# First keys in one VectorE instruction, two groups' keys spread from ScalarE's queue, the last down product in halves, and a new order of all pieces

## The reference

```python
x = x + attn_a(ln(x))   # W: 16 query heads, 2 key/value heads, window: query t sees keys t-16..t+15
x = x + ffn(ln(x))      # F: expand to 512, 9 butterfly stages, gelu, 9 butterfly stages, contract to 128
x = x + attn_b(ln(x))   # L: linear attention, phi = elu + 1
x = x + ffn(ln(x))      # G: the same weights as F
```

## Time and profile before

| | |
|---|---|
| runs of the kernel before | 549.33 us median of 3 (547.2, 549.33, 549.78) |
| profiled execution, its own time | 548.77 us |
| its span, first to last instruction | 547.0 us |
| TensorE busy | 514.8 us, 94% |
| GpSimd busy | 449.6 us, 82% |
| VectorE busy | 424.4 us, 78% |
| ScalarE busy | 356.5 us, 65% |
| granted TensorE clock | 0.999 |

### The profile page before, as it was taken

One profiled execution on the slowest core, in us unless ns is written; L12 is line 12 of the kernel. 1 busy time (PEld: TensorE's weight loads), 2 busy tenths in 40 slices (PEclk: granted clock), 3 DMA queues, 4 the chain that ended last, 5 costly groups with the idle time before them and its releaser, 6 DMA issues.

```text
span 547.0 us, 14353 instructions
## 1 busy us (share of the span) xinstructions
PE 514.8 (94%) x5060; PEld 337.4 (62%) x5060; DVE 424.4 (78%) x1272; ACT 356.5 (65%) x578; POOL 449.6 (82%) x640
## 2 busy tenths in 40 slices
PE   4788989999999999999999999999999999999996
PEld 2454344756667676666676676766576676767764
DVE  4978888997978888887888888888878687745451
ACT  2654457576768777776767686776777777747542
POOL 6548789999989999898998989999979796797240
PEclk9999999999999999999999999999999999999999
DMA  8433323231322212131423222231422312110001
GB/s 305 153 100 85 101 63 84 59 79 46 103 50 79 60 46 76 43 102 38 103 50 105 49 59 74 61 85 40 118 64 63 72 27 59 31 29 20 1 20 40
DMA packets 49543, 38.87 MB, mean 71 GB/s; under 512 B 12352, under 2 KB 38976, under 8 KB 49472
## 3 DMA queue, kind: packets, MB, share of 16 engines
q1 hardware_dynamic: 47024, 33.73, 24.4%
q10 hardware_dynamic: 2448, 4.22, 2.2%
HBM read 15.64 MB, written 5.51 MB: 39 GB/s over the span
## 4 chain that ended last, share of the span: by engine, by line
PE 61%; POOL 19%; DVE 5%; issue 5%; DMA 5%; SPq 3%; ACT 2%; POOLq 0%; DVEq 0%; ACTq 0%
PE ring L785 15%; PE ring L773 14%; POOL probs_t L602 7%; PE ring L715 6%; PE ps_s L741 6%; PE ring L796 4%; PE ps_o L758 4%; PE ring L816 3%; PE ring L866 2%; DMA probs_t<-probs_t 2%; SPq L446 2%; PE ring L843 2%; PE ring L805 1%; DMA x_P<-in_x 1%; POOL xb_W L572 1%
## 5 line engine op out<-in xcount | busy, mean ns | idle before, releaser
L602 POOL TENSOR_TENSOR probs_t<-probs_t,first 128x1024 f32<-128x1024 f32 x64 | 151.4, 2376 | 19.3 <-DMA probs_t<-probs_t 19.1
L785 PEld LDWEIGHTS ring<-w,early 128*128 128x128 f32 x1024 | 118.9, 192 | 10.8 <-issue 8.5
L1189 ACT ACTIVATE early<-ring,b 128x512 f32<-128x512 f32 x128 | 84.3, 685 | 62.2 <-PE ring L773 61.8
L785 PE MATMUL ring<-w,early 128*128 128x128 f32 x1024 | 119.8, 275 | 1.8 <-ACT early L1189 1.6
L1180 ACT ACT_TABLE_LOAD x58 | 74.4, 1283 | 10.1 <-issue 9.1
L1198 ACT ACTIVATE probs_t<-merged_t 128x1024 f32<-128x1024 f32 x64 | 65.8, 1044 | 11.4 <-DVE merged_t L1547 9.3
L741 PE MATMUL ps_s<-kx,q_t 64*32 64x512 f32 x960 | 64.7, 596 | 2.9 <-DVE merged L1540 1.6
L1555 DVE STREAM_TRANSPOSE ps_o<-ps_o 128x512 f32<-128x512 f32 x64 | 46.1, 721 | 21.3 <-PE ps_o L758 21.3
L773 PE MATMUL ring<-xT_G,w1b 128*128 128x512 f32 x128 | 60.8, 595 | 0.7 <-ACT xT_G L1170 0.7
L773 PE MATMUL ring<-xT_F,w1b 128*128 128x512 f32 x128 | 60.1, 608 | 0.4 <-ACT xT_F L1170 0.3
L1528 DVE COPY_PREDICATED ps_s<-first,ps_s 128x512 f32<-128x512 uint32 x64 | 43.9, 687 | 15.9 <-PE ps_s L741 14.7
(11 more groups left out here) (124 smaller groups left out, 985.7 us busy)
## 6 DMA issues: line engine op xcount, KB each, us to landing
probs_t<-probs_t SPq DMA_DIRECT2D x256, 64.0 KB, 2.0
kx<-kv_rows SPq DMA_DIRECT2D x120, 40.0 KB, 2.1
x_P<-in_x SPq DMA_DIRECT2D x16, 256.0 KB, 3.3
out_x<-x_G SPq DMA_DIRECT2D x16, 256.0 KB, 2.5
vx_t<-kv_rows SPq DMA_DIRECT2D x128, 8.0 KB
up_s<-in_up_m ACTq DMA_DIRECT2D x7, 256.0 KB, 7.9
down_s<-in_down_m ACTq DMA_DIRECT2D x7, 256.0 KB, 8.1
kv_rows<-kv_t SPq DMA_DIRECT2D x16, 80.0 KB, 2.8
```

The source lines that it names most:

```text
L602: nc.gpsimd.tensor_tensor(parts, parts, keep.rearrange("p (a t) -> p a t", a=1).to_broadcast([P, PAIR * HEADS, WIN]), ALU.mult).then_inc(p ...
L785: last = nc.tensor.matmul(bank(name)[:, P * j:P * (j + 1)], hid[s][:, c, P * j:P * (j + 1)], w2[:, c], start=(c == 0), stop=(c == CH - 1))
L1189: nc.scalar.activation(hid[s][:, c], bank(name)[:], ACT.Gelu, bias=b1[:, c:c + 1]).then_inc(drained[BANK[name]].sem, 1)
```

## The change

- **First keys.** The first half of group 0's keys (`X.ka`) is written by one VectorE instruction over 8 x 288 elements, with the head mask as a broadcast second operand; the second half (`X.kb`) by 8 ScalarE instructions. A new column `bk_row` holds the bias.
- **Clearing.** GpSimd clears half of `kx` (128x2560 instead of 128x5120), ScalarE the other half by one instruction (`clear_keys`). The ones of `v_ext` are set later.
- **Loads.** The 7 loads of `down_s` go out on SyncE's queue, behind `vx_t`, instead of between those of `up_s` on ScalarE's queue.
- **Keys of groups 1 and 2** (the second and third group) are spread by 8 DMAs each from ScalarE's queue; those of the other groups stay on SyncE's.
- **Last down product.** `G.down` of group 15 puts tiles 0 and 1 into the bank of its first hidden chunk, waits for each hidden chunk just ahead of its first use, and is followed by two residuals and two stores of 128 KB.
- **Order.** Every table and every `turn` is rewritten; the repeated stretch is now that of groups 4 to 12. Some results go to another bank: `W.proj` to `ring2` (was `ring1`), `L.xT` to `ring1` (was `ring0`).

```diff
-            nc.gpsimd.memset(kx[:], 0.0).then_inc(kx_cleared, 1)
-            nc.gpsimd.memset(v_ext[:], 1.0).then_inc(ones_set, 1)
+            nc.gpsimd.memset(kx[:, 0:HPK // 2], 0.0).then_inc(kx_cleared, 1)
+            def set_ones():
+                nc.gpsimd.memset(v_ext[:], 1.0).then_inc(ones_set, 1)
...
+            def spread_keys(g):
+                act.wait_ge(kv_out.sem, kv_out.after(g, "P.ko"))
+                if g == 1:
+                    act.wait_ge(kx_cleared, 2)
+                else:
+                    act.wait_ge(product.sem, product.after(g - 1, *SCORES))
+                for h in range(HPK):
+                    act.dma_start(kx[h:P:HPK, h].rearrange("d (j n) -> d j n", j=TILES), keys_of(g)
+                                 ).then_inc(kx_in.sem, 16)
...
+            def clear_keys():
+                act.wait_ge(kv_cleared, 1)
+                later_keys = kx[:, HPK // 2:HPK].rearrange("p h n -> p (h n)")
+                zeros = x_tp[:, 0:1, 0:PAD]
+                nc.scalar.activation(later_keys.rearrange("p (a n) -> p a n", n=PAD),
+                                     zeros.to_broadcast([P, HPK * TILES * TSPAN // (2 * PAD), PAD]), ACT.Copy).then_inc(kx_cleared, 1)
...
-                for h in range(HPK):
-                    last = nc.vector.tensor_scalar(kx_0[:, h, TPB * TSPAN + PAD:TILES * TSPAN - PAD],
-                                                   bank("X.kb")[:, PAD:TPB * TSPAN - PAD], head_s[:, h:h + 1],
-                                                   bk_head[:, h:h + 1], ALU.mult, ALU.add)
-                last.then_inc(drained[BANK["X.kb"]].sem, 1)
+                width = TPB * TSPAN - 2 * PAD
+                nc.vector.scalar_tensor_tensor(
+                    kx_0[:, :, PAD:TPB * TSPAN - PAD],
+                    bank("X.ka")[:, PAD:TPB * TSPAN - PAD].rearrange("p (a n) -> p a n", a=1).to_broadcast([P, HPK, width]), bk_row,
+                    head_s.rearrange("p (h a) -> p h a", a=1).to_broadcast([P, HPK, width]), ALU.add, ALU.mult
+                ).then_inc(drained[BANK["X.ka"]].sem, 1)
...
+                ends = ends_apart(g, s)
...
                 for j in range(TILES):
+                    if ends and j == TILES // 2:
+                        last.then_inc(first_tiles, 1)
+                        free(g, name)
+                    sums = bank(f"{s}.up{chunks[0]}" if ends and j < TILES // 2 else name)
+                    for c in chunks:
+                        if j == 0 and ends:
+                            ready = drained[BANK[f"{s}.up{c}"]]
+                            pe.wait_ge(ready.sem, ready.after(g, f"{s}.up{c}"))
...
-    ("P.xT", 0, "0", 0, 0), ("X.u0a", 0, "2", 0, 0), ("X.u0b", 0, "3", 0, 0), ("X.ka", 0, "0", 0, 0),
+    ("P.xT", 0, "0", 0, 0), ("X.u0a", 0, "1", 0, 0), ("X.u0b", 0, "2", 0, 0), ("X.ka", 0, "0", 0, 0),
```

More of the change, by code:

```diff
@@ L186 @@
+    ("P.kv", "bank"), ("P.q", "P.xT"), ("W.PV1", "values"), ("W.PV2", "values"), ("W.PV3", "values"), ("W.S1", "P.q"),
[8 rows of a table added]
 }
@@ L398, in first_loads @@
                              ).then_inc(vones_in, 16)
+                for m in reversed(range(INNER)):
+                    sp.dma_start(down_s[m][:], down_m[m]).then_inc(down_in[m], 16)
             def load_x(g):
@@ L488, in turn @@
[L488 to L501 removed]
+                    spread_keys(15)
@@ L1505, in residual @@
             def residual(g, s, name, base):
-                dve.wait_ge(product.sem, product.after(g, name))
+                ends = ends_apart(g, s)
+                dve.wait_ge(*((first_tiles, 1) if ends else (product.sem, product.after(g, name))))
                 if s == "G":
@@ L1514, in residual @@
                 own = drained[BANK[name]]
-                nc.vector.tensor_tensor(xs[s][:].rearrange("p j n -> p (j n)"), bank(name)[:],
-                                        xb_of(g, base)[:].rearrange("p j n -> p (j n)"), ALU.add).then_inc(own.sem, 1)
+                half = P * TILES // 2
+                rows, base_rows = [t[:].rearrange("p j n -> p (j n)") for t in (xs[s], xb_of(g, base))]
+                if ends:
+                    first_up = min((f"{s}.up{c}" for c in range(CH)), key=lambda up: product.after(g, up))
+                    nc.vector.tensor_tensor(rows[:, 0:half], bank(first_up)[:, 0:half], base_rows[:, 0:half], ALU.add
+                                            ).then_inc(first_rows, 1)
+                    dve.wait_ge(product.sem, product.after(g, name))
+                    nc.vector.tensor_tensor(rows[:, half:], bank(name)[:, half:], base_rows[:, half:], ALU.add
+                                            ).then_inc(own.sem, 1)
+                else:
+                    nc.vector.tensor_tensor(rows, bank(name)[:], base_rows, ALU.add).then_inc(own.sem, 1)
             def halves():
@@ new lines, in turn @@
+                if t == 3:
+                    residual(3, "W", "W.proj", "P")
+                    moments(3, "W")
+                    moments_joined(3, "W")
+                    residual(1, "L", "L.proj", "F")
+                if t == 2:
+                    phi_k_made(1, 1)
+                    phi_k_made(1, 0)
+                for g in due(t, 2, 0, 2):
+                    moments(g, "L")
+                if t == 2:
+                    phi_q_made(1)
+                    linear_state_out(1)
+                    moments_joined(0, "L")
@@ L1784, in turn @@
[L1784 to L1794 removed]
+                if t == 14:
+                    residual(14, "W", "W.proj", "P")
@@ L1877, in turn @@
-                for g in due(t, 60, 0, 12):
-                    residual(g, "G", "G.down", "L")
-                if t == 72:
+                if t == 11:
+                    merge_halves(13, 1)
+                for g in due(t, 0, 13, 14):
+                    moments(g, "W")
+                for g in due(t, 0, 4, 14):
+                    moments_joined(g, "W")
+                if t == 11:
+                    scores_transposed(13, 0)
+                for g in due(t, -1, 4, 14):
+                    heads_turned(g, 0)
@@ new lines, in turn @@
+                if t == 13:
+                    scores_transposed(15, 0)
+                if t == 12:
+                    heads_divided(13, 0)
+                if t == 5:
+                    moments(3, "L")
+                for g in due(t, 3, 0, 1):
+                    residual(g, "G", "G.down", "L")
+                for g in due(t, -4, 4, 13):
+                    moments(g, "P")
+                if t == 5:
+                    residual(2, "G", "G.down", "L")
+                if t == 2:
+                    linear_sums_inverted(1, 0)
@@ new lines, in turn @@
+                if t == 3:
+                    phi_q_made(2)
+                if t == 2:
+                    linear_divided(1, 0)
+                if t == 1:
+                    values_out(3)
+                    sums_inverted(2, 3)
+                    subtract_max(3, 3)
+                if t == 0:
+                    heads_divided(1, 2)
+                    residual(0, "F", "F.down", "W")
+                    heads_turned(1, 3)
+                    moments(0, "F")
+                    sums_inverted(1, 3)
+                    moments_joined(0, "F")
@@ new lines, in turn @@
+                if t == 0:
+                    values_out(2)
+                    scores_transposed(2, 3)
+                    merge_halves(3, 0)
+                    row_max(3, 0)
+                    residual(1, "W", "W.proj", "P")
+                    subtract_max(3, 0)
+                    moments(1, "W")
+                    heads_turned(2, 0)
+                    moments_joined(1, "W")
+                    scores_transposed(3, 0)
+                    merge_halves(3, 1)
+                for g in due(t, 127, 14):
+                    residual(g, "G", "G.down", "L")
@@ new lines, in turn @@
+                for g in due(t, -1, 13, 14):
+                    heads_divided(g, 2)
+                if t == 13:
+                    residual(13, "F", "F.down", "W")
+                    heads_turned(14, 3)
+                for g in due(t, 0, 4, 13):
+                    moments(g, "F")
+                    moments_joined(g, "F")
+                if t == 13:
+                    sums_inverted(14, 3)
+                for g in due(t, 1, 3, 12):
+                    linear_sums(g, 1)
+                if t == 13:
+                    values_out(15)
```

1841 lines of the change are left out of this document (1033 added, 808 removed), and 198 rows, old and new, of tables (COVERED, PARTED, PHI, PROBS).

## The result

The changed kernel takes **553.54 us** (median of 4 runs, 551.57 to 554.03) beside 549.13 (547.2 to 549.78) for the kernel before: a ratio of 1.0093, 95% interval [1.0063, 1.0124]. It is slower by 0.9%, where 542.9 and a range to 548.5 were predicted. Its profiled execution took 551.57 us, the shortest of the four; its span is 549.7.

What follows compares the result with a forecast made beforehand. TensorE was taken as the bound, busy 514.8 of 547.0 us, with GpSimd second. Gains of 2.5 (start), 2.4 (60 to 150 us) and 1.0 (end) sum to 5.9, so 548.77 becomes 542.9 us; range 538.5 to 548.5.

Steps and rivals of the forecast that it cites:

- Repeated stretch: Groups 4 to 12: no gain or loss if waits stay covered, 30.18 us a group as before.
- Rival 3: Repeated groups: the new order is slower, through a wait at `xb_L` or `ring1` exceeding GpSimd's 2.7 us room; 10%.
- The second outer stage (1.94) now stands ahead of the first merge: First spread: the stage takes 1.94 us, so the exponential is 2, not 3, us earlier.
- Transposes at 9.5, keys in one instruction of 2.55, S0(0) at 15.4: Start of group 0: transposes 2.0 us earlier, keys by one VectorE instruction, first score tile 3.0 us earlier.
- The keys of groups 1 and 2 on ScalarE, 2.5: First term, at the start: group 2's first score tile at 53.5, 2.5 us earlier; bounds 0 and 5.
- Rival 2: Start: ScalarE's stalls of about 5 us, twice, give the gain back; 545.5 to 549.5 us; 21%.
- GpSimd's lead, not TensorE's: First spreads of probabilities: maskings come 4 to 8 us earlier, a lead credited to GpSimd only.
- 60 to 150 us, 2.4: Second term: about half of TensorE's 4.75 us idle there goes, 2.4 us; bounds 0 and 4.75.
- End, 1.0: Third term: the last down product, residual and store in halves save 1.0 us; bounds 0 and 1.5.
- Sum: Whole kernel: 2.5 + 2.4 + 1.0 = 5.9 us gained, from 548.77 to 542.9 us.

Runs made afterwards that it cites:

- e11: The changed kernel with a third buffer for `xb_P` alone; `up_diag` still runs beside the outer stage: 546.75 us, ratio 0.9974.
- e8: The changed kernel with `up_diag` waiting for the second outer stage and a third buffer for `xb_P`: 542.25 us, ratio 0.9897.
- e12: e8 with the second group's key spread back on SyncE's queue, the third group's still on ScalarE: 549.28 us, ratio 1.0042.
- e6: e2 with the third group's key spread back on SyncE's queue, the second group's still on ScalarE: 551.42 us, ratio 1.0059.
- e2: The changed kernel with one more wait on GpSimd, `up_diag` made only after the second outer stage: 549.52 us, ratio 1.0037.
- e10: e8 with the last down product, its residual and its store whole again: 544.19 us, ratio 0.9924.
- e9: e8 with the third group's keys spread by SyncE and `X.wT` made ahead of `S0(2)`: 541.1 us, ratio 0.9869.

## Why the prediction was wrong, point by point

- *"Repeated stretch. Same pieces and table loads, a few neighbours swapped: 0, if the waits stay covered."* This step failed, and it is the sign of the result. One of the swapped neighbours, `xb_P` against `um1`, carries a wait into the chain from `x_W` to `xn_W`: 0.57 us a group, and 6.5 to 7.7 us in all, with the more costly first and last of these groups (e11, e8). Rival 3 was this case, and its kind of mechanism was right (an instruction of GpSimd ahead of what TensorE waits for), but it named `xb_L` and a bank, had 10%, and let the loss begin only when GpSimd's room of 2.7 us was used up. Room on the engine did not protect the chain: the group lengthened while GpSimd was idle 3.4 us in each 30.75.
- *"The second outer stage (1.94) now stands ahead of the first merge."* The duration failed: 5.3 us (1.19 + 4.15), since the change also moved `up_diag` beside it. In the kernel before, the stage had ended by 15.6, ahead of `up_diag` (17.96). With the overlap taken out the dates that follow are as predicted: E0(0)'s spread out at 21.6, first masking 25.83, second 33.33. It cost 3.1 to 4.2 us, the fall of the clock included. The Trainium skill has the rule (SBUF — State Buffer, "Who interferes with whom"): a VectorE instruction with two SBUF inputs contends with a GpSimd instruction that reads SBUF; the port pair they share is an exclusive lock, and the order of issue decides who is blocked. The traces agree: 1.12 us against 0.34 for the products that read `d_t` and `d_tmp`. Read against the new order of GpSimd, it would have given this term.
- *Transposes at 9.5, keys in one instruction of 2.55, S0(0) at 15.4.* Right: 9.0, 2.61 and 14.69.
- *The keys of groups 1 and 2 on ScalarE, 2.5.* In the changed kernel `S0(1)` and `S0(2)` came at 36.94 and 56.94, 0.3 and 0.9 later than the earlier trace rows, not at 35.0 and 53.5: the delay of the start came through. In e8 they are at 34.17 and 54.07. Rival 2 (the 5 us on ScalarE are given back) is refuted for the second group, as undoing the move costs 8.0 us (e12), part of it by the clock; for the third it is open, as SyncE in its place is 1.2 us slower, which is no clear difference (e6 against e2). The gain came another way than the term said. The prediction gave the earlier keys 1.6 us and called the 4 to 8 us of the maskings "GpSimd's lead, not TensorE's"; in e12 the keys are 0.4 us later, and it is the second masking for which TensorE stands 2.92 us. So most of what the move is worth seems to lie in SyncE's queue, which it frees for the probabilities. The transfers themselves got no faster: a key DMA landed after 2.4 us (median, `kx` in the changed kernel) from ScalarE's queue, after 2.1 from SyncE's.
- *60 to 150 us, 2.4.* About 2.0 in the changed kernel (4.75 to 2.8): right.
- *End, 1.0.* The term was too small, though within its bounds. The halves give 1.46 (e10). The changed kernel itself takes 10.33 us from its last up product to the end (539.37 to 549.7), where it was 11.79 (535.21 to 547.0).
- *Sum.* A gain of 5.9 us was predicted, to 542.9; with the two faults taken out, e8 gains 5.7 by its ratio (542.25 us, beside 547.69 for the kernel before in the same rounds). The gains were sized about right in sum, in part by luck. By the starts of the projections of q e8 is ahead of the kernel before by 2.4 us at group 3 (72.10 for 74.53), 5.3 at group 6 (147.34 for 152.62), 6.4 at group 15 (419.31 for 425.74) and 7.6 at the end of the span (539.4 for 547.0, the fastest execution of e8). So some 1.1 us came between groups 6 and 15, where the prediction saw nothing to gain. The two losses of 3 to 4 and 6.5 to 8 us were missed.

## What to carry to other kernels

When an order changes, walk each engine's queue at every wait of the repeated stretch: what stands between an arrival and the instruction that needs it can lengthen every iteration if the chain closes over them, even on an engine with idle time. Here 3.45 us of such work (1.09 + 2.36) made a group 0.57 us longer. Compare durations with what the other engine does in the new place, not in the old. And before a swapped piece is put back, ask what it frees: `xb_P` behind the norm cost 34 us, with a wait for a load in each group.

## What the runs showed of the hardware that was not expected

- VectorE's two-input products and GpSimd's go in step, one beside one, when both have four: each 0.34 us product takes 1.01 to 1.12, the four take 4.15 instead of 1.14, while GpSimd's four take 4.29 instead of 4.04.
- After a gap of TensorE of 2.4 to 3.2 us the granted clock was 0.50 for some 3 us (changed kernel, from 20.0, and e9) or 6 us (e2, from 52), and after another such gap it was not: behind the gap at 50 us neither in the profiled execution of the changed kernel (2.75 us idle) nor in that of e8 (2.66), but in that of e2 (2.92 us). In e12 it was at 0.50 for some 10 us, with a wait of 2.92 us inside. The mean clock differs between executions of one kernel, too (0.996 to 1.0 in the six of e9), and the lower ones cost 1.1 to 1.8 us there. Why it falls in one execution and not in the other stays open.
